# Pairing the attention products of both row halves in a cross-attention and FFN kernel

## The reference

```
B, N, D = 8, 100, 128        # batches, rows, width
M, C, H = 1444, 64, 16       # context rows, context width, heads

x = x + tanh(g_xattn[0]) * xattn(layernorm(x), ctx, Wq, Wk, Wv, Wo, bo)
x = x + tanh(g_ffn[0])   * ffn(layernorm(x), w_gate, w_up, w_down)

# xattn: softmax((q Wq)(ctx Wk)^T / 8) (ctx Wv), heads joined, times Wo, plus bo
# ffn:   fp4_linear(silu(fp4_linear(x, w_gate)) * fp4_linear(x, w_up), w_down)
```

## Time and profile before

| what | value |
|---|---|
| median of 3 runs | 607.21 us (606.7 to 607.94) |
| span of the profiled execution | 611.0 us |
| PE busy | 559.4 us (92%) |
| DVE busy | 470.2 us (77%) |
| ACT busy | 297.9 us (49%) |
| POOL busy | 276.4 us (45%) |
| mean granted TensorE clock | 0.959 |

### The profile page before, as it was taken

The page is one execution under the profiler, slowest core; times in us unless marked ns, Lnnn a source line. Parts: engine busy times, 40 slices in busy tenths (PEclk is TensorE's granted clock), DMA queues, the critical chain, the costliest instruction groups (busy, mean ns, idle before and its releaser), DMA issues.

```text
span 611.0 us, 10089 instructions
## 1 busy us (share of the span) xinstructions
PE 559.4 (92%) x2969; PEld 355.6 (58%) x2969; DVE 470.2 (77%) x793; ACT 297.9 (49%) x693; POOL 276.4 (45%) x234
## 2 busy tenths in 40 slices
PE   5988999999999997999999997999999999999742
PEld 4754665666575755666566664657566665646331
DVE  2769866789877994689967996779976998687655
ACT  3434645565456543465446643465455644546211
POOL 3027253644728271372826264282736265366500
PEclk9989999999999997999999999999999999999775
DMA  9400000200020000200030000200011000000000
GB/s 172 79 1 1 1 1 1 51 1 1 5 52 2 1 1 13 50 2 1 1 56 2 1 0 13 49 2 1 1 38 20 2 0 5 1 0 1 1 4 4
DMA packets 27922, 9.71 MB, mean 16 GB/s; under 512 B 24016, under 2 KB 27600, under 8 KB 27856
## 3 DMA queue, kind: packets, MB, share of 16 engines
q1 hardware_dynamic: 27856, 8.92, 7.6%
HBM read 8.50 MB, written 0.41 MB: 15 GB/s over the span
## 4 chain that ended last, share of the span: by engine, by line
PE 73%; DVE 21%; issue 3%; ACT 1%; DMA 1%; POOL 0%; SPq 0%; POOLq 0%; DVEq 0%; ACTq 0%
PE attn L788 21%; PE scores L774 14%; PE ring L727 10%; PE scores L775 9%; DVE max L894 6%; PE ring L706 5%; PE ring L734 4%; PE ring L741 3%; DVE f_abs L362 2%; DVE rsum L901 2%; DVE f_abs L364 2%; DVE e_gate L859 2%; PE ring L747 2%; PE ring L713 1%; DVE h_fp L366 1%
## 5 line engine op out<-in xcount | busy, mean ns | idle before, releaser
L633 ACT ACTIVATE probs<-scores 120x400 f32<-120x400 f32 (+1 forms) x384 | 190.0, 504 | 238.5 <-PE scores L775 236.7
L894 DVE TENSOR_REDUCE max<-ring 116x1 f32<-116x482 f32 (+1 forms) x336 | 205.0, 648 | 39.3 <-PE ring L727 36.8
L505 POOL TENSOR_TENSOR acc_p<-acc_p,probs 120x800 f32<-120x800 f32 x79 | 156.3, 1978 | 66.4 <-ACT probs L633 62.8
L788 PE MATMUL attn<-probs,ctx_n 120*64 120x400 f32 (+1 forms) x768 | 174.5, 534 | 0.0
L774 PE MATMUL scores<-q_hh,k_hl 128*120 128x400 f32 (+1 forms) x384 | 154.4, 402 | 6.2 <-issue 5.1
L774 PEld LDWEIGHTS scores<-q_hh,k_hl 128*120 128x120 f32 (+1 forms) x384 | 70.8, 184 | 132.1 <-ACT probs L633 70.3
L775 PE MATMUL scores<-q_ls,k_h 71*120 71x400 f32 (+1 forms) x384 | 134.7, 351 | 0.0
L727 PE MATMUL ring<-k_hl,q_hh 128*116 128x482 f32 (+1 forms) x336 | 121.6, 414 | 6.2 <-DVE max L894 5.7
L775 PEld LDWEIGHTS scores<-q_ls,k_h 71*120 71x120 f32 (+1 forms) x384 | 71.6, 186 | 4.2
L727 PEld LDWEIGHTS ring<-k_hl,q_hh 128*116 128x116 f32 (+1 forms) x336 | 58.9, 181 | 15.1 <-DVE max L894 7.7
L788 PEld LDWEIGHTS attn<-probs,ctx_n 120*64 120x64 f32 (+1 forms) x768 | 38.4, 136 | 47.4 <-issue 35.2
(11 more groups left out here) (126 smaller groups left out, 514.3 us busy)
## 6 DMA issues: line engine op xcount, KB each, us to landing
ctx_n<-in_ctx SPq DMA_DIRECT2D x16, 360.0 KB
wq<-in_L_xattn_Wq SPq DMA_DIRECT2D x1, 512.0 KB, 4.7
wo<-in_L_xattn_Wo SPq DMA_DIRECT2D x1, 512.0 KB, 7.6
x_in<-in_x SPq DMA_DIRECT2D x8, 50.0 KB
out<-y_out SPq DMA_DIRECT2D x8, 50.0 KB
wk<-in_L_xattn_Wk SPq DMA_DIRECT2D x1, 256.0 KB, 4.0
ctx_n<-in_ctx SPq DMA_DIRECT2D x16, 1.0 KB
wv<-in_L_xattn_Wv SPq DMA_DIRECT2D x1, 256.0 KB, 6.4
```

What stands on the lines that cost most here:

```text
L505: pool.tensor_tensor(acc_p[0:r, t.g % 2, :], left, probs[0:r, c % PROBS, :], ALU.add).then_inc(sum_p, 1)
L633: act.activation(probs[0:r, c % PROBS, k * HALF:(k + 1) * HALF], scores[0:r, slot % SCORE_BANKS, 0:HALF], ACT.Exp).then_inc(probs_full, 1)
L788: mm = pe.matmul(attn[64 * i:64 * i + C, k, 0:HALF], ctx_n[0:r, par, c, 0, :], probs[0:r, c % PROBS, k * HALF:(k + 1) * HALF], start=(j == ...
L894: dve.tensor_reduce(max3[0:rows, tile, part:part + 1], src[0:rows, 0:MAXC[part + 1] - MAXC[part]], AX.X, ALU.max).then_inc(free, 1)
```

## The change

The two halves of a chunk pair are issued together. `attn_pairs(t, j, back)` loops over `k` and issues four products; it stands in slot 4j+5 (`PAIR_SLOT = 1`), after the scores and ring items of that slot. Half 0 is thereby issued one slot later and half 1 one slot earlier. The two copies of `attn` on ACT move from slots 1 and 3 to 2 and 3. The products themselves, their operands and their semaphores are the same.

```
+PAIR_SLOT = 1
+COPY_SLOTS = [2, 3]
...
-                    if t.g >= 1 and slot in (1, 3):
-                        copy_attn(t, slot // 2)
+                    if t.g >= 1 and slot in COPY_SLOTS:
+                        copy_attn(t, COPY_SLOTS.index(slot))
...
-            def attn_pair(t, i, back):
...
+            def attn_pairs(t, j, back):
...
                 par = (t.g - back) // 2 % 2
-                pe.wait_ge(probs_full, t.count(SLOTS, 4 * j + 3 + k - SLOTS * back))
-                if j == 0 and t.g >= 1:
-                    pe.wait_ge(attn_copied, t.count(2, k - 1))
-                for i in (1, 0):
...
+                for k in range(2):
+                    pe.wait_ge(probs_full, t.count(SLOTS, 4 * j + 3 + k - SLOTS * back))
+                    if j == 0 and t.g >= 1:
+                        pe.wait_ge(attn_copied, t.count(2, k - 1))
+                    for i in (1, 0):
...
-                    if slot % 2 == 0:
-                        i = slot // 2 - 2
-                        if i >= 0:
-                            attn_pair(t, i, 0)
+                    if slot % 4 == PAIR_SLOT:
+                        j = slot // 4 - 1
+                        if j >= 0:
+                            attn_pairs(t, j, 0)
                         elif t.g >= 1:
-                            attn_pair(t, i + CHUNKS, 1)
+                            attn_pairs(t, j + CHUNKS // 2, 1)
...
-                for i in (CHUNKS - 2, CHUNKS - 1):
-                    attn_pair(t, i, 1)
+                attn_pairs(t, CHUNKS // 2 - 1, 1)
```

More of the change, by code:

```diff
@@ L775, in score_slot @@
                 pe.matmul(dst, k_h1[par][0:C + TILES, a:a + r], q_ls[0:C + TILES, half, cols], start=False, stop=True).then_inc(scores_full, 1)
-            def attn_pair(t, i, back):
-                j, k = i // 2, i % 2
+            def attn_pairs(t, j, back):
                 par = (t.g - back) // 2 % 2
-                pe.wait_ge(probs_full, t.count(SLOTS, 4 * j + 3 + k - SLOTS * back))
-                if j == 0 and t.g >= 1:
-                    pe.wait_ge(attn_copied, t.count(2, k - 1))
-                for i in (1, 0):
[L786 to L790, removed]
+                for k in range(2):
[3 more added lines that the diff above has]
+                    for i in (1, 0):
+                        c = 2 * j + i
+                        r = CROWS[c]
+                        mm = pe.matmul(attn[64 * i:64 * i + C, k, 0:HALF], ctx_n[0:r, par, c, 0, :], probs[0:r, c % PROBS, k * HALF:(k + 1) * HALF],
+                                       start=(j == 0), stop=(j == CHUNKS // 2 - 1))
+                    mm.then_inc(pv_done, 1)
             def group(t):
```

## The result

The changed kernel takes 644.57 us (median of 4 runs, 643.12 to 645.9) against 607.58 us: a ratio of 1.0575, 95% interval 1.0517 to 1.0632. The forecast was slower, 614 us, at most 625. The direction came out and the size did not.

A forecast was written before the change was run, and what follows sets the result against it. PE paces nearly everywhere, DVE in odd groups' slots 6 to 18. Even groups +3.0, odd +4.2, group 0 -0.1, group 1 -1.0, group 14 -0.1, group 15 +0.4: about +6.5, giving 614 us; own range 608.5 to 622, overall 601 to 625.

The forecast's parts named there:

- Joining saves 0.34 us a time: Attn blocks on PE: two apart cost 1.01 us each, the second joined 0.67; 32 us saved in all.
- The stalls that take it back: Even groups, slots 0, 4 and 5, 11, 16, 21: PE waits sum to 2.55 us against 2.05 saved.
- the restart of 0.10 us: After a stall, PE's next score product follows 0.28 us behind instead of 0.18, costing 0.10 more.
- an even group was to lose 0.50 us: Per even group: stalls of 2.55 us against 2.05 saved by joining; 3.0 us over groups 2 to 12.
- h_fp comes about 1.0 us later: Odd groups: later `sum` and a slot 11 stall pass through DVE's full stretch to the FP4 step `hT` awaits.
- I had 0.57: Odd groups, slot 6: `sum` comes 0.57 us later, as PE issues four pairs before it instead of three.
- the stall of slot 11: Second `max` waits for the bank of the second `proj`: 0.47 us with restart; in odd groups it starves DVE.
- Rival C: Slower: `hT` wait grows to about 2.0 us, clock falls, 8 to 17 us on top: 622 to 631; chance 0.12.
- B: Faster: DVE's slack in odd groups absorbs the later `sum` and slot 11's stall: 601 to 606 us; chance 0.12.
- D: PE the only bound, no stall: 575 us, or 591 with half the saving; chance 0.05.
- The odd group, forecast 0.7 us longer: `h_fp` about 1.0 us later, less 0.34 given back in slots 20 to 22; 4.2 us over groups 3 to 13.

The follow-up runs named there:

- slots 2, 6, 10: Changed kernel with the joined blocks one slot later (slots 2, 6, 10, 14, 18, 22): 608.72 us, ratio 0.9906 to the kernel before.
- the runs with small additions: POOL's additions cut to one column: in the kernel before 584.17 us (ratio 0.9599), in the changed kernel 593.33 us (0.9761).
- the longer delay of `sum`: Kernel before, blocks not joined, eight extra products (1.75 us) ahead of `sum` in six odd groups: 623.7 us, ratio 1.0231.
- the filled kernel: Changed kernel with eight extra products (1.8 us together) ahead of PE's wait for `hT` in odd groups: 631.3 us, ratio 1.032.

## Why the prediction was wrong

**Right.** Joining saves 0.34 us a time (a joined block costs 1.68 us). The stalls that take it back are real and stand where the prediction has them, and the restart of 0.10 us is there. Their size was too low: an even group was to lose 0.50 us, and group 12 lost 0.92; over all even groups the mean is 0.5 only because the one behind the first loop turn got 1.5 us shorter, which nothing in the prediction says. That the position, not the joining, does the harm shows in slots 2, 6, 10.

**The step that failed: "h_fp comes about 1.0 us later".** PE's first product on `h_fp` starts 33.61 us into group 11 (467.61 - 434.00) instead of 30.64 (443.85 - 413.21), so 3.0 us later. Of this, 0.84 us is there when DVE takes its first step on `sum` (I had 0.57). The other 2.1 us are DVE's own: between that step and `h_fp` its timeline marks no idle time, so the stall of slot 11, which I had down for 0.47, starved nothing. Line 352 grew by 1.4 us, 360 by 1.5 and 356 by 0.6, 362 shrank by 0.7, and smaller shifts make up the sum; the three that grew ran beside an instruction of POOL. I had carried DVE's lengths over unchanged. The earlier trace rows showed DVE full, and I read full as paced by its own work; part of that fullness was waiting for POOL, inside the instructions' own time, and I had not asked why a step on 8 numbers (line 901) lasts 1.78 us.

The Trainium skill's page "SBUF — State Buffer", section "SBUF: two separate sides", says that VectorE and GpSimd share one pair of ports under an exclusive lock, held for a whole instruction; on VectorE's side it concerns instructions in a 2-port mode or with two inputs in SBUF. The DVE steps that end 0.03 and 0.20 us after POOL's additions, and the runs with small additions, agree with it. The traces show who ends with whom and not the lock itself.

**Rival C came true, and I gave it 0.12 and too low a price.** I had put the half clock at 8 to 17 us on top of a wait of 2.0 us. The wait was 2.46 to 2.48 us and the clock fell in all six odd groups of the changed kernel. Filling it gave back 15.5 us, within the 8 to 17; the errors were the chance, and the total of 622 to 631 us, which left out the longer DVE steps.

**The sum.** Of the 37 us, the change costs about 9 where POOL's additions are small, and the half clock about 15.5 (the filled wait, with the new falls in slot 8 counted in). The remaining 12 or so I put down to the longer DVE steps; that is what is left over, and no run measures it by itself. The three need not be independent, since the small additions also shorten the wait that sets the clock. Group 11 gives a second reading: of its 5.7 us, 0.7 come in slots 0 to 5, 2.4 up to the end of the wait for `hT`, and 2.6 in the slots at half clock.

**Rivals B and D** fell: nothing was absorbed, and PE was not alone in setting the pace. The odd group, forecast 0.7 us longer, is 5.7 longer in group 11 and 5.1 on average.

## What to carry to other kernels

Before moving work on the engine that sets the pace, look at what each piece hides on the others: here blocks of 1 us in each second slot hid the round trip over two score banks and the emptying of a bank, and one slot's shift (4j+6 in place of 4j+5) turns a loss of 5.8% into a gain of about 1%. An instruction that lasts several times its usual time in a trace may be waiting inside itself, as lines 355 and 363 did here; look at what the other engines do at that moment before its length is carried into a forecast. In this kernel a delay of 0.88 us of `sum` came out as nothing, and one of 0.84 us went with an `h_fp` 3.0 us later.

## What the runs showed of the hardware

- A DVE step that starts during one of POOL's additions of 1.9 us lasts until it is over: 1.54 us on 22 numbers a partition, 1.88 on 352, against 0.16 and 0.33. Counted over the 13 traces, with more than 0.25 us of the addition left: 42 TENSOR_SCALAR steps on 352 numbers (the form of L363) ended 0.20 to 0.21 us after it, and 140 steps with two inputs from SBUF (the forms of L365 and L367) 0.38 to 0.39 after it.
- Not affected beside the same additions: the `max` reductions that read PSUM (0.62 to 0.66 us), and the reciprocals on 22 numbers (40 cases, 0.27 to 0.28 us).
- The granted clock fell to half (1.2 GHz) behind an idle PE of 2.48 us in one group and stayed at 2.4 GHz behind the same idle time in another group of the same run. In the changed kernel it fell behind all six waits of 2.46 to 2.48 us. Behind 2.12 us (the longer delay of `sum`) and 2.45 us (`PAIR_SLOT = 2`) it fell in four of six groups each. Behind 1.12 us it stayed up in the kernel before, yet in slot 8 of the filled kernel it fell behind 0.63 us, so the length of one wait does not settle it. 1.8 us of useless products in the wait for `hT` kept it up behind that wait, worth 15.5 us in the changed kernel.
- Four f32 attn products in two column halves, back to back, take 1.49 us to the next product's start at full clock. Two blocks of two cost 2 x 1.01 us and one block of four 1.68 us, so standing apart costs 0.34 us more.
